# The last expert weights are split by GpSimd behind the row scatter, and TensorE waits for one expert's weights at a time

## The reference, cut to what matters

```
gate_weights = softmax(x @ Wg + bg)             # 1024 rows, 8 experts
topv, topi = top_k(gate_weights, 2)
h = gelu(x @ W1[n] + b1[n])                     # 256 -> 512
h = gelu(h @ W2[n] + b2[n])                     # 512 -> 512
eo = h @ W3[n] + b3[n]                          # 512 -> 256
out = sum over the two chosen experts of topv * eo
```

## Time and profile before

| | before |
|---|---|
| median of 3 runs | 732.91 us (731.61 to 738.06) |
| the profiled execution's own time | 732.86 us |
| its span, first to last instruction | 731.0 us |
| PE busy | 561.6 us (77%) |
| DVE busy | 433.2 us (59%) |
| ACT busy | 299.7 us (41%) |
| POOL busy | 254.8 us (35%) |

### The profile page before, as it was taken

How to read it: one execution, slowest core, us unless ns; L and a number is a source line. 1 busy time by engine, 2 the same in 40 slices (tenths; PEclk the granted TensorE clock), 3 DMA queues, 4 the chain that set the end, 5 groups by cost and what they waited for, 6 DMA issues and landing times.

```text
span 731.0 us, 12063 instructions
## 1 busy us (share of the span) xinstructions
PE 561.6 (77%) x4143; PEld 396.7 (54%) x4143; DVE 433.2 (59%) x994; ACT 299.7 (41%) x742; POOL 254.8 (35%) x297
## 2 busy tenths in 40 slices
PE   3948799167289999999977989889888467764765
PEld 2537344155169989777634647566576245543333
DVE  3586899955645554444474553535555656767674
ACT  1511200243533443433343744816564355545553
POOL 3950478845600000000378863917612200010000
PEclk9979899755689999999999999999999789996796
DMA  8592310555641111110230000000000500000000
GB/s 289 183 370 92 127 58 0 172 163 183 205 171 59 34 56 45 38 31 23 59 108 0 1 1 1 1 0 1 1 1 1 172 1 3 2 2 0 7 22 30
DMA packets 32248, 49.62 MB, mean 68 GB/s; under 512 B 3096, under 2 KB 22368, under 8 KB 31808
## 3 DMA queue, kind: packets, MB, share of 16 engines
q1 hardware_dynamic: 29888, 41.65, 17.1%
q0 software_dynamic: 2304, 7.21, 2.8%
HBM read 39.68 MB, written 9.18 MB: 67 GB/s over the span
## 4 chain that ended last, share of the span: by engine, by line
PE 50%; POOL 15%; DVE 15%; ACT 11%; issue 4%; DMA 3%; SPq 0%; ACTq 0%; DVEq 0%; POOLq 0%
PE bank L1559 15%; PE bank L1574 4%; PE bank L1722 4%; POOL sm L523 3%; POOL rq L516 3%; POOL sorted_rows L498 3%; POOL qs L518 2%; POOL rq L514 2%; ACT pT L818 2%; PE bank L1437 2%; PE bank L1967 2%; DVE xn L924 2%; PE bank L1866 2%; PE bank L1466 1%; PE bank L1468 1%
## 5 line engine op out<-in xcount | busy, mean ns | idle before, releaser
L666 ACT ACTIVATE hf<-bank,be 128x256 f32<-128x256 f32 (+1 forms) x120 | 44.3, 420 | 75.3 <-PE bank L1559 59.1
L1559 PE MATMUL bank<-h,wsp 128*128 128x256 f16 (+1 forms) x720 | 72.5, 250 | 2.6 <-DVE h L1117 1.4
L504 POOL DMA_INDIRECT yg<-expert_rows,pos x16 | 15.8, 989 | 164.9 <-DMA expert_rows<-yb 160.3
L1559 PEld LDWEIGHTS bank<-h,wsp 128*128 x720 | 60.6, 97 | 13.7 <-issue 4.8
L1115 DVE CAST h<-hf 128x512 f16<-128x512 f32 (+1 forms) x60 | 21.9, 365 | 64.0 <-ACT hf L666 63.1
L486 POOL TENSOR_TENSOR kvp<-xnT,cxT 128x512 f32<-128x512 f32 x32 | 35.6, 1135 | 43.2 <-issue 33.3
L721 ACT ACTIVATE sm<-sm,nm 128x128 f32<-128x128 f32 x128 | 49.8, 393 | 1.0 <-DVE nm L1230 1.0
L576 ACT CAST wsp<-wraw 128x2048 f16<-128x2048 f32 x12 | 22.7, 1900 | 65.8 <-DMA wraw<-in_L_ffn_W 65.8
L464 POOL TENSOR_TENSOR wsp<-wraw,wsp 128x512 f16<-128x512 f32 x40 | 45.8, 1177 | 9.1 <-ACT wsp L576 8.8
L1227 DVE SCALAR_TENSOR_TENSOR sm<-bank,const 128x512 f32<-128x512 f32 x32 | 22.1, 691 | 38.6 <-PE bank L1689 38.6
L523 POOL TENSOR_TENSOR sm<-sm,rinv 128x512 f32<-128x512 f32 x32 | 33.1, 1040 | 24.3 <-DVE rinv L1221 24.3
(11 more groups left out here) (299 smaller groups left out, 1314.7 us busy)
## 6 DMA issues: line engine op xcount, KB each, us to landing
wraw<-in_L_ffn_W SPq DMA_DIRECT2D x16, 512.0 KB, 5.2
wraw<-in_L_ffn_W SPq DMA_DIRECT2D x8, 1024.0 KB, 5.9
cxT<-in_ctxT SPq DMA_DIRECT2D x2, 1024.0 KB, 7.5
tap<-in_taps SPq DMA_DIRECT2D x1, 2048.0 KB, 14.3
xg<-sorted_rows SPq DMA_DIRECT2D x8, 256.0 KB, 3.1
expert_rows<-yb SPq DMA_DIRECT2D x8, 256.0 KB, 2.2
sorted_rows<-early POOLq DMA_DIRECT2D x1, 1536.0 KB, 12.0
sorted_rows<-early POOLq DMA_DIRECT2D x1, 1408.0 KB, 15.3
```

The lines of the kernel that those rows point to most:

```text
L666: last = nc.scalar.activation(hf[:, p, n * k:n * k + n], bank[2 * (layer - 1) + p][:, n * k:n * k + n], ACT.Gelu, bias=be[:, layer - 1, u, ...
L1559: last = nc.tensor.matmul(b[:, n * (f % 2):n * (f % 2) + n], w[a_][:, c, P * f:P * f + P], inp[:, b_, c, :], start=(c == 0 and a_ + b_ == ...
```

## The change

DVE's six subtracts go, and with them `w_split_dve`. POOL subtracts half 10 ahead of the scatter with the others (`EARLY_LOWS` is 11). Behind the scatter, once PE's preparation is done, it subtracts 11 and 12, and casts and subtracts 13, 14 and 15 (`split_both`), in pieces as the first four. ACT casts 4 to 12 only. SP loads halves 13 and 14 behind the rows of tiles 0 and 1, half 15 behind the rows of tile 2, and wqb, wkvT, the biases and cxT only behind the store of tile 3; ACT's copy into wqb moves from the first tile to the end of tile 2, behind a wait for all splits. PE waits, ahead of layer 1 of each tile, until that tile's expert is split, against a value computed from the register with its number.

```diff
+EARLY_LOWS = 11
 expert_half(e, half):
-                if 2 <= k < 12:
+                if k >= 2:
                     sp.wait_ge(sem("w_split"), k - 1)
-                elif k >= 12:
-                    sp.wait_ge(sem("w_split_dve"), k - 11)
...
-                    if e >= 2:
+                    if 2 <= e and 2 * e + half <= EARLY_LOWS + 1:
                         expert_half(e, half)
...
             for j in range(2):
                 rows_in(j)
+            for k in range(EARLY_LOWS + 2, 2 * NE - 1):
+                expert_half(k // 2, k % 2)
...
-            sp.wait_ge(sem("w_split_dve"), 6)
-            sp.dma_start(wqb[:, :, 1] ...), wkvT, bv5, bk5; wait wab_moved; cxT
             for j in range(ET):
                 if j + 2 < ET:
                     sp.wait_ge(sem("xgT_psum"), j + 1)
                     rows_in(j + 2)
+                if j == 0:
+                    expert_half(NE - 1, 1)
                 rows_out(j)
+                if j == 3:
+                    sp.wait_ge(sem("w_split"), 2 * NE)
+                    sp.dma_start(wqb[:, :, 1] ...), wkvT, bv5, bk5; wait wab_moved; cxT
... POOL
+                elif k > EARLY_LOWS + 1:
+                    pool.wait_ge(sem("w_hi_pool"), POOL_HALVES + k - EARLY_LOWS - 1)
...
-            for k in range(POOL_HALVES, 10):
+            for k in range(POOL_HALVES, EARLY_LOWS):
                 split_low(k)
...  (the scatter)
+            pool.wait_ge(sem("prep4_psum"), 8)
+            for k in range(EARLY_LOWS, EARLY_LOWS + 2):
+                split_low(k)
+            for k in range(EARLY_LOWS + 2, 2 * NE):
+                split_both(k)
... ACT
             prep(0, 2)
-            split_high(12); prep(2, 4); split_high(13); prep(4, 8); split_high(14); split_high(15)
+            for k in range(12, EARLY_LOWS + 2):
+                split_high(k)
+            prep(2, 8)
...
                 expert_out(j)
+                if j == 2:
+                    act.wait_ge(sem("w_split"), 2 * NE)
+                    nc.scalar.copy(wqb[:, :, 0] ..., wab ...).then_inc(sem("wab_moved"), 1)
... DVE
-            for k in range(10, 14):
-                split_low(k)
             (adds of b3)
-            split_low(14)
-            split_low(15)
... PE
+            def weights_ready(e):
+                pe.wait_ge(sem("w_split"), e * 2 + 2)
-            pe.wait_ge(sem("w_split"), 10)
-            pe.wait_ge(sem("w_split_dve"), 6)
             e_next = expert_of(0)
+            weights_ready(e_next)
             layer(1, 0, e_next)
             for j in range(ET):
                 e, e_next = e_next, expert_of(j + 1) if j + 1 < ET else None
                 layer(2, j, e)
                 if j + 1 < ET:
+                    weights_ready(e_next)
                     layer(1, j + 1, e_next)
```

More of the change, by code:

```diff
@@ L430, in _ @@
                     rows_in(j + 2)
+                if j == 0:
+                    expert_half(NE - 1, 1)
                 rows_out(j)
+                if j == 3:
+                    sp.wait_ge(sem("w_split"), 2 * NE)
+                    sp.dma_start(wqb[:, :, 1].rearrange("p c h n -> p c (h n)"), a["wqb_rope"].rearrange("p (c n) -> p c n", c=3)).then_inc(sem("w4_loaded"), 16)
+                    sp.dma_start(wkvT[:], a["wkvT"].rearrange("(c p) n -> p c n", p=P)).then_inc(sem("context5_loaded"), 16)
+                    sp.dma_start(bv5[:], a["L1_xattn_bkv"][D:2 * D].partition_broadcast(P)).then_inc(sem("context5_loaded"), 16)
+                    with nc.allow_non_contiguous_dma(reason="one value per partition"):
+                        sp.dma_start(bk5[:], a["L1_xattn_bkv"][0:D].rearrange("(c p) -> p c", p=P)).then_inc(sem("context5_loaded"), 16)
+                    sp.wait_ge(sem("wab_moved"), 1)
+                    sp.dma_start(cxT[:].rearrange("p c t s -> p (c t s)"), a["ctxT"]).then_inc(sem("cxT_loaded"), 16)
             sp.wait_ge(sem("l3_psum"), ET)
@@ L465, in split_low, with split_both @@
                 last.then_inc(sem("w_split"), 1)
-            for k in range(POOL_HALVES):
+            def split_both(k):
                 pool.wait_ge(sem("w_loaded_odd" if k % 2 else "w_loaded_even"), (16 if k % 2 else 32) * (k // 2 + 1))
@@ L473, in _ @@
                 split_low(k)
+            for k in range(POOL_HALVES):
+                split_both(k)
             pool.wait_ge(sem("zeroed"), 1)
@@ L677, in _ @@
             hidden(1, 0)
-            act.wait_ge(sem("w_split_dve"), 6)
-            nc.scalar.copy(wqb[:, :, 0].rearrange("p c h n -> p c (h n)"), wab[:].rearrange("p c h n -> p c (h n)")).then_inc(sem("wab_moved"), 1)
             for j in range(ET):
@@ L684, in _ @@
                 expert_out(j)
+                if j == 2:
+                    act.wait_ge(sem("w_split"), 2 * NE)
+                    nc.scalar.copy(wqb[:, :, 0].rearrange("p c h n -> p c (h n)"), wab[:].rearrange("p c h n -> p c (h n)")).then_inc(sem("wab_moved"), 1)
             nc.scalar.preload_act_table_set("natural_log_exp_and_others")
```

## The result

The changed kernel is slower by half a per cent: the ratio of its times to those of the kernel before, run in turn on the same chip, is 1.0052, with an interval of 1.0033 to 1.0072, some 3.8 us. Its median is 739.02 us (20 runs) beside 734.35 (20 runs); they lie 4.7 us apart, inside the ratio's interval (2.4 to 5.3 us). The ratio leaves out one execution of the kernel after, of 746.76 us, in which the chip was in a slower state. The profiled execution took 736.37 us (span 734.6), 3.5 over that of before. The end of the expert stage, the first matmul of the key and value products behind it, moved from 353.11 to 356.46 us, so nearly all of the loss lies in the stretch that the prediction spoke of. Lines of the kernel after stand up to 14 higher than before, those of SP's row loads and stores one lower.

A forecast was written before the change was run, and what follows sets the result against it. The prediction took the path from routing through POOL's scatter to the first expert tile, then PE's tiles, as the bound. Terms -3.6 + 2.5 + 1.2 + 1.0 = +1.1 us on 732.86 gave 734.0 us, range 728.5 to 740.

The forecast's parts named there:

- rival 2: Expert tiles: DVE becomes the bound while POOL works, over three tiles; 9.2 lost in place of 3.7, 739.5 us; chance 0.13.
- the late loads: SP's queue: wqb, wkvT, biases and cxT stand ahead of tile 6's rows and delay them; +1.0 us, bounds 0 to 1.7.
- the register waits: PE, ahead of the tiles: 15 waits for expert weights, queued ahead of its stream, cost nothing; at worst 0.2 us each.
- The scatter: POOL's 16 row-scatter DMAs: waiting for DVE's weight splits ends when those go; -7.3 us, bounds 0 to 7.3.
- The third rival: Scatter: the change does not shorten it, the long DMAs having another cause; 741.3 us; chance 0.05.
- The routing: Ahead of the scatter: four DVE instructions each wait out a piece of POOL's subtract 10; +3.7 us, bounds 0 and 4.5.
- Tiles 0 and 1: DVE's hidden-layer splits alternate with POOL's late pieces: +2.5 us in tile 0, +1.2 from tile 0 to 1.
- the first rival: Tiles: DVE's instructions slip into POOL's gaps, so only the 3.6 us earlier start is left; 729.3 us; chance 0.22.
- The rest at nothing: Tiles: ACT's wqb copy, ACT's wait on all 16 splits and late weights needed after 250 us, each priced at 0.

The follow-up runs named there:

- dve_dummy: Changed kernel plus six unused 128x2048 SBUF-to-SBUF subtracts on DVE beside the scatter, without weight loads; 750.55 us (one run).
- extra_loads: Changed kernel plus five extra 512 KB loads from HBM beside the scatter, no more DVE work; 740.12 us (one run).
- late10: Changed kernel with subtract 10 on POOL behind the scatter instead of ahead of it; 737.49 us (12 runs), ratio 1.0042 to the kernel before.
- no_late: Changed kernel without loads and splits of halves 12 to 15, experts 6 and 7 using expert 5's weights; 737.88 us.
- fine: Changed kernel with POOL's late casts and subtracts in pieces of 256 columns instead of 512; 733.72 us (one run).
- rows_first: Changed kernel with the loads of wqb, wkvT, biases and cxT behind tile 6's rows; 734.89 us (12 runs), ratio 1.0012 to the kernel before.
- const_waits: Changed kernel with PE's waits for expert weights against constants instead of a register's value; 732.91 us (one run).
- best: Changed kernel with late10, rows_first, fine, register waits for the first eight tiles only, ACT's wqb copy one tile later; 731.70 us, ratio 0.9959 to the kernel before.

## Why the prediction came out as it did

**The place and the kind of each priced term were right; one of them was mis-sized, and a cost that was put at nothing was there.** The forecast of 734.0 was 1.1 over the profile before; the ledger gives 3.3, and the ratio some 3.8. The median of 739.02 lies near the upper end of the range of 728.5 to 740, and above the 731 to 737 that the forecast gave itself; on the 732.86 it started from, the ratio would make 736.7. That rival 2's 739.5 stands closer to the median is chance, as its condition did not come true. One of the prediction's own signs went against it: it called itself wrong if the tile stage lost over 7 us, and the stage lost 7.15 (152.15 to 159.30) where 4.7 was forecast. Of the 2.4 more, 1.9 are the late loads and 0.8 the register waits; tile 0 lost 0.3 less.

*The scatter (-7.3).* Right, and its cause is shown: dve_dummy brings 6.2 of it back, extra_loads nothing. The rule that spoke against it, the Trainium skill, "SBUF — State Buffer", section "Who interferes with whom", infers that a DVE tensor_tensor does not hold up the writing of GpSimd's DMA descriptors. The measurement decides against the forecast that I had drawn from it, a scatter no shorter than before: 0.96 becomes 1.86 to 2.03 under each subtract. Whether it is the writing that waits is not shown, as an indirect DMA also reads its positions (`pos`), and I had not asked which of the two is held up. The third rival rested on that use of the rule and falls.

*The routing (+3.7).* Right: four of the routing's short instructions wait for most of a POOL piece each, 3.3 in all, and late10 takes 3.2 of it away. Which four was a guess: L1066, which I had counted, does not wait, and one of the two of L1071 does.

*Tiles 0 and 1 (+2.5, +1.2).* Right: 2.16 and 1.23. The turns that I built from rows of the layer norm and the first halves, 1.35 for a cast and 1.6 for a subtract, came out at 1.37 and 1.52. no_late takes both away but for 0.2, and fine 2.5 of the 3.4. So the first rival (DVE slips into the gaps) falls by rows, and so does the second (DVE bounds three tiles): POOL was through at 227.0, as forecast.

*The late loads ahead of tile 6's rows (+1.0, 0 to 1.7): the step that failed.* It measured 2.92, and rows_first takes out 2.85. I let the rows be asked for at 258 and land between 263.2, 5.2 us later like the row load of the earlier trace rows, and 266; they were asked for at 258.60, took 8.3 and landed at 266.9. The upper bound let SP's issuing hide 5.2 of the 8 us that I had put on the 1.4 MB more that stand ahead. No row stood behind that, and SP's issues were some 3 us long by my own count (3.84 measured). What stayed was 3.1 us, and the cxT load took 8.7 us where the same load in front of the earlier trace rows took 4.8. The wait of 2.34 is not all either: layer 2 began 0.86 us after the start of the transposes instead of 0.44. The price was thus above the upper bound that I gave it.

*The register waits (0, at worst 0.2 each).* The reason for 0, that they are queued ahead of PE's stream, fits the big tiles and fails for the small ones: 0.12 to 0.14 each, shown by const_waits.

*The rest at nothing* (ACT's copy, its new wait, the late weights): no row of after shows a wait at them.

**What is not settled.** The granted clock fell behind the second wait for h in tile 0 in the profiles of late10 (1.92 us), dve_dummy (1.92) and best (1.78). It did not in those of after, extra_loads and rows_first (1.92 each) and const_waits (1.88), where the 42 matmuls took 4.75 or 4.76. What tells the two groups apart is open. Whether other executions of the kernel after have such a fall, and so the half microsecond between its ledger and its ratio, is open too: only one execution was recorded.

## What to carry to other kernels

Work that was moved from VectorE to GpSimd cost here what it held up, not what it took: find the first stretch in which VectorE's chain is exposed (here the routing and tile 0), keep GpSimd's large pieces out of it by one wait, and cut the rest small. When an engine is made to wait, follow the buffer that it holds to the queue that loads it, and see what stands behind that load; here a row load behind 2.4 MB cost 2.9 us, and one behind a held buffer 7.5. Do not count what is queued ahead of a load as hidden unless a row shows it.

## What the runs showed of the hardware that I had not expected

- Halving GpSimd's piece brought VectorE's subtract of 0.69 us from 1.52 to 1.04 beside GpSimd's subtracts and from 0.98 to 0.76 beside its casts, and POOL's own end only from 227.0 to 233.4.
- The granted clock, just risen to 1.0 (2.4 GHz), went back to 0.5 (1.2 GHz) behind waits of 1.78, 1.92 and 1.92 us in layer 2 of tile 0 (best, late10, dve_dummy): 42 matmuls took 6.32, 6.42 and 7.66 us instead of 4.76. So a wait there cost 1.9 to 2.5 times its length, but in four other profiles no more than itself.
- A wait on a semaphore against a register's value cost PE 0.12 to 0.14 us in the tiles of 128 rows, one against a constant 0.02 or less.
